# Four eight-product pairs ahead of the first seven-product pair, one behind the last, and variance 1 of the last group's first columns formed on VectorE

## The chip, the cores and the metric

The kernel runs on one core of one Trainium2 chip. The metric is device time in microseconds (us) of the whole launch. The profiler's trace comes from one execution.

## The reference

A batch of 1024 x 10240 values is split in two halves of 5120 columns. Each half goes through two linear layers with layer norm and a leaky ReLU; the two results are put side by side, go through a third such layer, and a last product gives one number per row.

```python
F = 5120
x1, x2 = (x[:, :F], x[:, F:])                      # x: (1024, 10240)
h1 = leaky_relu(layer_norm(x1 @ W1.T))             # W1: (256, 5120)
h2 = leaky_relu(layer_norm(x2 @ W1.T))
h1 = leaky_relu(layer_norm(h1 @ W2.T))             # W2: (64, 256)
h2 = leaky_relu(layer_norm(h2 @ W2.T))
h = jnp.concatenate([h1, h2], axis=-1)
h = leaky_relu(layer_norm(h @ W3.T))               # W3: (8, 128)
return h @ W4.T                                    # W4: (1, 8)
```

`leaky_relu(x) = max(0.05 x, x)`; `layer_norm` subtracts the row's mean and divides by its root of the variance. The first layer is nearly all of the work.

## The kernel before, in words

**Tiling.** The rows are handled in two groups (`g` 0 and 1) of 512 rows, and a group in two batches (`b` 0 and 1) of 256 rows; with both column halves a batch is 512 columns of the moving operand (NC). The 5120 features are 20 pairs of 2 x 128. A product is 128 x 128 weights by 128 x 512 columns, accumulated in one of eight PSUM banks.

**Units.** A unit is one pair of features of one group. An ordinary unit (kind E) has eight products: two halves c (`parts`, buffers E0 and E1, of two blocks of x each) by two batches by two blocks of outputs. A seven (kind S) does a 2 x 2 block product with seven products, three on raw blocks of x (part R) and four on sums of blocks (part T). H and L are E units whose halves use the buffer T; F is the first E of group 1; D is the last two E units together. The string `ORDER` gives the kinds in order for each group; `plan()` numbers the units and their parts.

**Three passes.** Each product is done in three matmuls, since x and the weights are split in a high part (rounded to fp32r) and a low part (the rest): lo x hi, hi x lo, hi x hi. So an E unit is 24 matmuls, an S unit 21. ScalarE makes the high parts (`hi`, L587; weights in L547 and L571), VectorE the low parts (`lo`, L705; weights in L727 and L713). TensorE first takes the high x high products of a part, then waits for the low part.

**Weights.** Weights are read once, in group 0 (and for the two sevens more that group 1 has, nth 12 and 13). ScalarE takes their mean (L541, two for a unit), centres them (L547, two), and for a seven VectorE forms four sums (L739, L744, L749) before ScalarE casts `ws_hi` (L571) and VectorE makes `ws_lo` (L713). A ring of three slots takes the raw weights, so weight n + 3 is loaded after weight n is used up.

**x.** Halves of E units are loaded into a ring of four slots (`load_half`, L406), raw blocks of sevens into a ring of two (L379). The sums of a seven's x (L760, L770, L776) are made on VectorE; for the third to the sixth seven, a DMA that adds makes two of them.

**Order.** Every engine runs its instructions in the order in which they are written. The loop over `RUNS` writes it: a run `es` is the units between one seven and the next, `n` is the seven that follows, `after` the next run. For the first run (`i == 0`) the order is written apart, and also for the run that crosses from group 0 to group 1 (`crosses`). SP's loads are in the same order, each waiting for the low part that frees its slot; a few loads at the start are written out by hand.

**Ends.** After the last unit of a group layer 1 is leaked and squared on ScalarE, squares are summed over the two output blocks on VectorE (`sum_squares`, L834; `sum_last_squares`, L829), and layer 2 follows on TensorE (L1128). In group 1 four small matmuls (eight records, L1141, `sum_variance1`) with a vector of ones sum the squares over partitions, so that the variance has rows on partitions. For batch 0 they stand between layer 2 of batch 0 and TensorE's last block of batch 1 (`last_two`). `variance1` takes the reciprocal and a copy of that, `variance2` forms var12 = var2 x (1/var1) x var1 (L843, L844), GpSimd the power of -1/2 (`root12`, L484), `layer3` the third layer and its variance (L855, L857), GpSimd `root3` (L489), then `layer4` and the output. For group 0 the variances travel by GpSimd's DMAs (L505 to L526), and its end on VectorE stands where `first_end` says, within the sevens of group 1.

## Time and profile before

| | us |
|---|---|
| median of 3 runs | 232.28 |
| lowest and highest | 231.49, 232.99 |
| the profiled execution | 232.81 |
| its span in the trace | 231.0 |
| TensorE busy in it | 224.3 |
| VectorE busy | 191.1 |
| ScalarE busy | 151.7 |

The trace's times count from the span's start. What lies around the span is 232.81 - 231.0 = 1.8 us. In the trace PE is TensorE's matmuls and PEld its weight loads, DVE is VectorE, ACT ScalarE, POOL GpSimd, SP the engine that issues most DMAs. A matmul's end is modelled and overlaps with its successor, so starts are compared, not ends. The granted clock of TensorE is 0.99 of its full 2.4 GHz over the span.

### The profile page before, as it was taken

What the parts mean: (1) busy time and instruction counts of PE and PEld (TensorE: products, weight loads), DVE (VectorE), ACT (ScalarE), POOL (GpSimd) and SP (SyncE); (2) the same over time, 40 slices, a digit from 0 to 9 for tenths busy, and PEclk for the clock granted to TensorE, in tenths of its full rate; (3) what the DMA queues carried; (4) which work ended last, traced back from release to release, by engine and by line L of the source; (5) the groups of instructions that cost most, each with busy time, mean ns of one, the idle gap of its engine ahead of it and who ended that gap; (6) DMA issues with size and microseconds to landing.
All of it is one profiled execution on the core that took longest, in us unless ns stands there. A gap on an engine that the chain in (4) does not pass through costs nothing.

```text
span 231.0 us, 2894 instructions
## 1 busy us (share of the span) xinstructions
PE 224.3 (97%) x999; PEld 179.2 (78%) x999; DVE 191.1 (83%) x245; ACT 151.7 (66%) x240; POOL 28.8 (12%) x41
## 2 busy tenths in 40 slices
PE   8999999999999999999999999999999999999991
PEld 3678776888888888888878888888888878888771
DVE  4589999968869999996669699999989699979324
ACT  5797989779498598963688363665546484824630
POOL 0000020020200200000012243237001400000014
PEclk9999999999999999999999999999999999999996
DMA  6999999999999999556738958668776414150000
GB/s 201 390 407 403 378 318 281 335 289 348 319 234 348 276 295 301 184 166 226 275 65 235 296 176 269 220 208 224 246 246 245 139 74 131 53 182 1 3 0 1
DMA packets 17950, 51.93 MB, mean 225 GB/s; under 512 B 2772, under 2 KB 3156, under 8 KB 17936
## 3 DMA queue, kind: packets, MB, share of 16 engines
q1 hardware_dynamic: 15920, 48.60, 61.5%
q0 software_dynamic: 1872, 2.89, 7.7%
q10 hardware_dynamic: 144, 0.26, 0.3%
q8 instruction: 8, 0.13, 0.3%
q14 instruction: 6, 0.05, 0.1%
HBM read 50.95 MB, written 0.01 MB: 221 GB/s over the span
## 4 chain that ended last, share of the span: by engine, by line
PE 82%; DMA 5%; DVE 4%; ACT 4%; issue 1%; POOL 1%; SPq 1%; POOLq 0%; DVEq 0%
PE acc L1006 79%; DMA xe_raw<-x 5%; PE acc L1128 2%; DVE xe_lo L705 2%; ACT xe_hi L587 2%; ACT unused L541 1%; DVE x_sum L760 1%; PE acc L1141 1%; ACT xt_hi L587 1%; DVE x_sum L770 1%; ACT we_hi L547 0%; POOL inv L484 0%; ACT stage L547 0%; PE acc L1149 0%; PE acc L1157 0%
## 5 line engine op out<-in xcount | busy, mean ns | idle before, releaser
L1006 PE MATMUL acc<-xe_lo,we_hi 128*128 128x512 f32 x176 | 68.9, 391 | 0.3 <-DVE xe_lo L705 0.2
L1006 PE MATMUL acc<-xe_hi,we_lo 128*128 128x512 f32 x176 | 68.6, 390 | 0.0
L705 DVE TENSOR_TENSOR xe_lo<-xe_raw,xe_hi 128x1024 fp32r<-128x1024 f32 (+1 forms) x48 | 55.5, 1177 | 14.5 <-ACT xe_hi L587 14.5
L587 ACT CAST xe_hi<-xe_raw 128x1024 fp32r<-128x1024 f32 (+1 forms) x48 | 47.9, 1010 | 29.5 <-PE acc L1006 22.1
L1006 PE MATMUL acc<-xe_hi,we_hi 128*128 128x512 f32 x176 | 48.3, 391 | 0.0
L1006 PEld LDWEIGHTS acc<-xe_lo,we_hi 128*128 128x128 f32 x176 | 33.1, 188 | 8.4 <-issue 1.7
L1006 PEld LDWEIGHTS acc<-xe_hi,we_hi 128*128 128x128 f32 x176 | 32.9, 188 | 7.4 <-issue 0.7
L1006 PEld LDWEIGHTS acc<-xe_hi,we_lo 128*128 128x128 f32 x176 | 33.1, 188 | 6.7
L587 ACT CAST xt_hi<-x_sum 128x2048 fp32r<-128x2048 f32 x14 | 26.8, 1911 | 12.7 <-DVE x_sum L776 12.7
L705 DVE TENSOR_TENSOR xt_lo<-x_sum,xt_hi 128x2048 fp32r<-128x2048 f32 x14 | 32.0, 2288 | 1.9 <-ACT xt_hi L587 1.9
L1006 PE MATMUL acc<-xt_lo,ws_hi 128*128 128x512 f32 x64 | 25.0, 391 | 0.1
L1006 PE MATMUL acc<-xt_hi,ws_lo 128*128 128x512 f32 x64 | 24.9, 390 | 0.0
L705 DVE TENSOR_TENSOR xr_lo<-xs_raw,xr_hi 128x1536 fp32r<-128x1536 f32 x14 | 24.5, 1751 | 0.0
L587 ACT CAST xr_hi<-xs_raw 128x1536 fp32r<-128x1536 f32 x14 | 20.7, 1476 | 5.8 <-PE acc L1006 5.8
L1006 PE MATMUL acc<-xt_hi,ws_hi 128*128 128x512 f32 x64 | 17.1, 390 | 0.0
L1006 PE MATMUL acc<-xr_lo,ws_hi 128*128 128x512 f32 x42 | 16.6, 396 | 0.0
L1006 PE MATMUL acc<-xr_hi,ws_lo 128*128 128x512 f32 x42 | 16.4, 390 | 0.0
L571 ACT CAST ws_hi<-stage 128x896 fp32r<-128x896 f32 x8 | 7.6, 946 | 12.7 <-DVE stage L749 12.7
L541 ACT ACTIVATE unused<-stage 128x256 bf16<-128x256 f32 x39 | 15.8, 407 | 0.0
L1006 PEld LDWEIGHTS acc<-xt_lo,ws_hi 128*128 128x128 f32 x64 | 12.0, 188 | 3.2 <-issue 0.5
L1006 PEld LDWEIGHTS acc<-xt_hi,ws_hi 128*128 128x128 f32 x64 | 11.9, 188 | 2.7 <-issue 0.2
L496 POOL DMA_DIRECT2D x_sum<-x x4 | 5.0, 1256 | 71.7 <-DMA x_sum<-x 71.7
(107 smaller groups left out, 274.1 us busy)
## 6 DMA issues: line engine op xcount, KB each, us to landing
xe_raw<-x SPq DMA_DIRECT2D x51, 512.0 KB, 5.0
xs_raw<-x SPq DMA_DIRECT2D x14, 768.0 KB, 5.8
stage<-w SPq DMA_DIRECT2D x21, 256.0 KB, 5.8
x_sum<-x SPq DMA_DIRECT2D x10, 256.0 KB, 3.9
x_sum<-x SPq DMA_DIRECT2D x4, 512.0 KB, 4.2
x_sum<-x POOLq DMA_DIRECT2D x4, 512.0 KB, 8.8
stage<-w SPq DMA_DIRECT2D x2, 128.0 KB, 3.1
xe_raw<-x ACTq DMA_DIRECT2D x1, 256.0 KB, 3.2
```

Of the source, the lines that this page charges most:

```text
L496: pool.dma_start(x_sum[:, s, 0:2 * NC].rearrange("p (a n) -> p a n", a=2), b12_of(u).rearrange("p (o n) -> p o n", o=1).broadcast_to([P, 2 ...
L541: act.activation(unused[:, c, :], w_raw[:, s, c * N1:(c + 1) * N1], ACT.Copy, scale=-1.0 / N1, accum_out=w_mean[:, u.pair, c:c + 1]).then_ ...
L571: act.copy(ws_hi[:, u.pair, :], w_mid[:, P:]).then_inc(w_hi_ready, 1)
L587: act.copy(hi_of(u, part), raw_of(u, part)).then_inc(hi_ready[part.buffer], 1)
L705: dve.tensor_tensor(lo_of(u, part), raw_of(u, part), hi_of(u, part).bitcast(F32), ALU.subtract)\
L760: dve.tensor_tensor(x_sum[:, s, 0:2 * NC].rearrange("p (a n) -> p a n", a=2), raw[:, 0:3:2, :], b12, ALU.add).then_inc(two_sums_made, 1)
L770: dve.tensor_tensor(x_sum[:, s, 2 * NC:3 * NC], x_sum[:, s, 0:NC], x_block(u, 2), ALU.add)\
L1006: return pe.matmul(acc[:, bank, :], w, x, start=first, stop=True, skip_group_check=True)
L1128: ins = pe.matmul(h2_ps[b][h * N2:(h + 1) * N2, :], w2_sb[:, m, :], a1[:, b, m, h * T * P:(h + 1) * T * P], start=(m == 0), stop=(m == M - ...
L1141: ins = pe.matmul(acc[:, var1_bank[g][b], k:k + 1], sq1_sum[b][:, j * P:(j + 1) * P], ones[:], start=True, stop=True)
```

## The change

It does four things.

1. Group 0 runs E H E E S E E S ... S E L instead of E H E S E E S ... S E E L: one eight-product unit moves from behind the last seven to ahead of the first. ScalarE, VectorE and SP are written to match; the run that crosses the groups is one unit shorter. The load of w2, w3, w4 goes with its unit (W23_UNIT).
2. `first_end`, the end of group 0 on VectorE, moves one run earlier (SEVEN + 4 instead of SEVEN + 5).
3. In group 1, batch 0, the sums of squares over partitions leave TensorE: VectorE transposes blocks of 32 x 32, reduces over 32, moves the quarters side by side, reduces them, and takes reciprocal and product.
4. var12 = var2 x `cancelled`, where `cancelled` = (1/var1) x var1 is formed ahead. In layer 3 a square with accumulated output for each of the column tiles replaces a square and a reduce.

```diff
-W23_UNIT = 7
-ORDER = ("EHE" + "SEE" * 3 + "SE" * 2 + "SEEL", "FE" + "SE" * 8 + "D")
+W23_UNIT = 8
+ORDER = ("EHEE" + "SEE" * 3 + "SE" * 2 + "SEL", "FE" + "SE" * 8 + "D")
...
             load_w_after(UNITS[1])
             load_halves(UNITS[1], 0)
             load_halves(UNITS[1], 1)
-            load_seven(1)
-            load_two(1)
             load_w_after(UNITS[2])
             load_halves(UNITS[2], 0)
             load_halves(UNITS[2], 1)
+            load_seven(1)
+            load_two(1)
+            load_w_after(UNITS[3])
+            load_halves(UNITS[3], 0)
+            load_halves(UNITS[3], 1)
...
                     if i == 0:
                         hi(es[2], es[2].parts[0])
+                        start_w(es[3])
                         hi(es[2], es[2].parts[1])
                         start_w(n)
                     hi(n, n.parts[0])
-                    for j, u in enumerate(es[1:] if i else [], 1):
+                    for j, u in enumerate(es[1:] if i else es[3:], 1):
...
+            def cancel(a, b):
+                dve.tensor_tensor(cancelled[:, a * J:b * J], var1_inverse[:, a * J:b * J], var1[:, a * J:b * J], ALU.mult)\
+                    .then_inc(cancelled_ready, 1)
+
+            def variance1_of_first_columns():
+                turned = h1[0][1]
+                dve.wait_ge(sq1_summed, B * (GROUPS - 1) + 1)
+                step(dve.transpose(turned, sq1_sum[0]))
+                step(dve.tensor_reduce(quarter_sums[:], turned.rearrange("p (n f) -> p n f", f=Q32), AX.X, ALU.add))
+                for q in range(4):
+                    ins = dve.tensor_copy(side_by_side[:, :, q], quarter_sums[q * Q32:(q + 1) * Q32, :])
+                step(ins)
+                for q in range(4):
+                    rows = side_by_side[:].rearrange("p (h t r) q -> p h t r q", h=H, t=T)[:, :, :, q, :]
+                    ins = dve.tensor_reduce(var1[q * Q32:(q + 1) * Q32, 0:J].rearrange("p (t h) -> p h t", t=T), rows,
+                                            AX.X, ALU.add)
+                step(ins)
+                step(dve.reciprocal(var1_inverse[:, 0:J], var1[:, 0:J]))
+                cancel(0, 1)
...
             def variance2(n, a, b, summed):
-                step(dve.tensor_tensor(var2[:, a * J:b * J], summed, var1_inverse[:, a * J:b * J], ALU.mult))
-                dve.tensor_tensor(var12[:, a * J:b * J], var2[:, a * J:b * J], var1[:, a * J:b * J], ALU.mult)\
+                dve.wait_ge(cancelled_ready, n)
+                dve.tensor_tensor(var12[:, a * J:b * J], summed, cancelled[:, a * J:b * J], ALU.mult)\
                     .then_inc(var12_ready, 1)
...
-                step(dve.scalar_tensor_tensor(out=sq3[:, t], in0=h3[:, t], scalar=1.0 / N3, in1=h3[:, t],
-                                              op0=ALU.mult, op1=ALU.mult))
-                dve.tensor_reduce(var3[:, t], sq3[:, t], AX.X, ALU.add).then_inc(var3_ready, 1)
+                for k in range(a * T, b * T):
+                    ins = dve.scalar_tensor_tensor(out=sq3[:, k], in0=h3[:, k], scalar=1.0 / N3, in1=h3[:, k],
+                                                   op0=ALU.mult, op1=ALU.mult, accum_out=var3[:, k:k + 1])
+                ins.then_inc(var3_ready, 1)
...
                     seven_into(g, 0)
+                    lo(es[1], es[1].parts[0])
                     seven_into(g, 1)
-                    w_lo(es[2])
-                    lo(es[1], es[1].parts[0])
+                    lo(es[1], es[1].parts[1])
                     seven_into(g, 2)
                     seven_into(g, 3)
-                    lo(es[2], es[2].parts[0])
-                    lo(es[1], es[1].parts[1])
-                    lo(es[2], es[2].parts[1])
-                    for part in es[3].parts:
-                        lo(es[3], part)
+                    for part in es[2].parts:
+                        lo(es[2], part)
...
                     lo(es[1], es[1].parts[1])
                     lo(es[2], es[2].parts[0])
+                    w_lo(es[3])
                     lo(es[2], es[2].parts[1])
                     sums(n)
+                    lo(es[3], es[3].parts[0])
                     lo(n, n.parts[0])
+                    lo(es[3], es[3].parts[1])
...
-                first_end = n.nth == SEVEN + 5
+                first_end = n.nth == SEVEN + 4
...
             sum_squares(g, 0)
-            variance1(1, 0, 1, var1_ps(g, 0, 1))
+            variance1_of_first_columns()
             sum_last_squares()
             dve.wait_ge(var2_summed, 1)
             variance2(2, 0, 1, var2_ps(g, 0, 1))
-            variance1(2, 1, 2, var1_ps(g, 1, 2))
+            variance1(1, 1, 2, var1_ps(g, 1, 2))
...
                     if m == 0:
                         layer2(u.g, 0, range(M))
-                        sum_variance1(u.g, 0)
```

**The order near the start.** VectorE's rows from the low part of the third unit's first half (xe0_lo) on, first of the kernel before; L739, L760, L744, L770, L749 and L776 are the sums for the first seven, xr_lo and xt_lo its low parts.

```order
L705 TENSOR_TENSOR xe0_lo<-xe_raw,xe0_hi 128x1024
L705 TENSOR_TENSOR xe1_lo<-xe_raw,xe1_hi 128x1024
L739 TENSOR_TENSOR stage<-stage 128x256
L760 TENSOR_TENSOR x_sum<-xs_raw,x_sum 128x1024
L744 SCALAR_TENSOR_TENSOR stage<-stage 128x128
L770 TENSOR_TENSOR x_sum<-x_sum,xs_raw 128x512
L749 TENSOR_TENSOR stage<-stage 128x128
L776 TENSOR_TENSOR x_sum<-x_sum,xs_raw 128x512
L705 TENSOR_TENSOR xr_lo<-xs_raw,xr_hi 128x1536
L713 TENSOR_TENSOR ws_lo<-stage,ws_hi 128x896
L705 TENSOR_TENSOR xt_lo<-x_sum,xt_hi 128x2048
L727 SCALAR_TENSOR_TENSOR we_lo<-stage,w_mean,we_hi 128x256 x2
```

And of the changed kernel, where L710 is L705, L732 is L727, L744 to L781 the sums:

```order
L710 TENSOR_TENSOR xe0_lo<-xe_raw,xe0_hi 128x1024
L732 SCALAR_TENSOR_TENSOR we_lo<-stage,w_mean,we_hi 128x256 x2
L710 TENSOR_TENSOR xe1_lo<-xe_raw,xe1_hi 128x1024
L744 TENSOR_TENSOR stage<-stage 128x256
L765 TENSOR_TENSOR x_sum<-xs_raw,x_sum 128x1024
L749 SCALAR_TENSOR_TENSOR stage<-stage 128x128
L775 TENSOR_TENSOR x_sum<-x_sum,xs_raw 128x512
L754 TENSOR_TENSOR stage<-stage 128x128
L781 TENSOR_TENSOR x_sum<-x_sum,xs_raw 128x512
L710 TENSOR_TENSOR xe0_lo<-xe_raw,xe0_hi 128x1024
L710 TENSOR_TENSOR xr_lo<-xs_raw,xr_hi 128x1536
L710 TENSOR_TENSOR xe1_lo<-xe_raw,xe1_hi 128x1024
```

The fourth unit's weight part (L732 x2) comes between the third unit's halves; its own low parts (the second xe0_lo and xe1_lo) stand behind the first seven's sums, and with the seven's raw low part between them. Before, they stood behind all of that seven. ScalarE at the same place, before (L541 means, L547 centring, L587 casts of x, L571 cast of a seven's weights):

```order
L587 CAST xe0_hi<-xe_raw 128x1024
L587 CAST xe1_hi<-xe_raw 128x1024
L541 ACTIVATE unused,w_mean<-stage 128x256 x2
L547 ACTIVATE stage<-stage,w_mean 128x256 x2
L587 CAST xr_hi<-xs_raw 128x1536
L571 CAST ws_hi<-stage 128x896
L587 CAST xt_hi<-x_sum 128x2048
L541 ACTIVATE unused,w_mean<-stage 128x256 x2
```

and in the changed kernel (L548, L554, L594, L578):

```order
L594 CAST xe0_hi<-xe_raw 128x1024
L548 ACTIVATE unused,w_mean<-stage 128x256 x2
L554 ACTIVATE we_hi<-stage,w_mean 128x256 x2
L594 CAST xe1_hi<-xe_raw 128x1024
L548 ACTIVATE unused,w_mean<-stage 128x256 x2
L554 ACTIVATE stage<-stage,w_mean 128x256 x2
L594 CAST xr_hi<-xs_raw 128x1536
L594 CAST xe0_hi<-xe_raw 128x1024
L578 CAST ws_hi<-stage 128x896
L594 CAST xt_hi<-x_sum 128x2048
L594 CAST xe1_hi<-xe_raw 128x1024
```

The fourth unit's means and centrings come ahead of xe1_hi of the third, and its casts xe0_hi and xe1_hi before and behind the first seven's ws_hi and xt_hi.

**The end of group 0 on VectorE.** Before, around L966 to L869, with the seven of new weights (L739 to L713) behind it:

```order
L864 TENSOR_TENSOR weighted<-a3,w4_sb 128x32
L865 TENSOR_REDUCE y_sum<-weighted 128x4
L705 TENSOR_TENSOR xe1_lo<-xe_raw,xe1_hi 128x1024
L869 TENSOR_TENSOR y<-y_sum,inv3 128x4
L739 TENSOR_TENSOR stage<-stage 128x256
L760 TENSOR_TENSOR x_sum<-xs_raw,x_sum 128x1024
L744 SCALAR_TENSOR_TENSOR stage<-stage 128x128
L770 TENSOR_TENSOR x_sum<-x_sum,xs_raw 128x512
L749 TENSOR_TENSOR stage<-stage 128x128
L776 TENSOR_TENSOR x_sum<-x_sum,xs_raw 128x512
L705 TENSOR_TENSOR xr_lo<-xs_raw,xr_hi 128x1536
L713 TENSOR_TENSOR ws_lo<-stage,ws_hi 128x896
```

In the changed kernel the same rows, y (L900) and what is behind it, up to the seven with new weights (L744):

```order
L896 TENSOR_REDUCE y_sum<-weighted 128x4
L710 TENSOR_TENSOR xe1_lo<-xe_raw,xe1_hi 128x1024
L900 TENSOR_TENSOR y<-y_sum,inv3 128x4
L765 TENSOR_TENSOR x_sum<-xs_raw,x_sum 128x1024
L775 TENSOR_TENSOR x_sum<-x_sum,xs_raw 128x512
L781 TENSOR_TENSOR x_sum<-x_sum,xs_raw 128x512
L710 TENSOR_TENSOR xr_lo<-xs_raw,xr_hi 128x1536
L710 TENSOR_TENSOR xt_lo<-x_sum,xt_hi 128x2048
L710 TENSOR_TENSOR xe0_lo<-xe_raw,xe0_hi 128x1024
L710 TENSOR_TENSOR xe1_lo<-xe_raw,xe1_hi 128x1024
L744 TENSOR_TENSOR stage<-stage 128x256
L765 TENSOR_TENSOR x_sum<-xs_raw,x_sum 128x1024
```

A seven without weight rows and its eight now stand between the two.

**The last block.** TensorE between the two last blocks, before (L1128 layer 2, L1141 the variance sums):

```order
L1006 MATMUL acc<-xe1_lo,we_hi 128x512
L1006 MATMUL acc<-xe1_hi,we_lo 128x512
L1128 MATMUL acc<-x_sum,w2_sb 64x256 x4
L1141 MATMUL acc<-ones,stage 128x1 x4
L1006 MATMUL acc<-xe0_hi,we_hi 128x512
L1006 MATMUL acc<-xe0_lo,we_hi 128x512
```

and in the changed kernel (L1159 layer 2, L1038 products):

```order
L1038 MATMUL acc<-xe1_lo,we_hi 128x512
L1038 MATMUL acc<-xe1_hi,we_lo 128x512
L1159 MATMUL acc<-x_sum,w2_sb 64x256 x4
L1038 MATMUL acc<-xe0_hi,we_hi 128x512
L1038 MATMUL acc<-xe0_lo,we_hi 128x512
L1038 MATMUL acc<-xe0_hi,we_lo 128x512
```

The row of four matmuls with the vector of ones is gone. VectorE behind the last sum of squares (L834), before:

```order
L834 TENSOR_TENSOR stage<-stage 128x512
L838 RECIPROCAL var1_inverse<-acc 128x4
L839 COPY var1<-acc 128x4
L829 TENSOR_TENSOR stage<-stage,xs_raw 128x256 x2
L843 TENSOR_TENSOR var2<-acc,var1_inverse 128x4
L844 TENSOR_TENSOR var12<-var2,var1 128x4
L838 RECIPROCAL var1_inverse<-acc 128x4
L839 COPY var1<-acc 128x4
L843 TENSOR_TENSOR var2<-acc,var1_inverse 128x4
L844 TENSOR_TENSOR var12<-var2,var1 128x4
L852 TENSOR_TENSOR half3<-acc,inv12 128x32
```

and in the changed kernel (L839):

```order
L839 TENSOR_TENSOR stage<-stage 128x512
L859 STREAM_TRANSPOSE stage<-stage 128x512
L860 TENSOR_REDUCE quarter_sums<-stage 128x16
L862 COPY side_by_side<-quarter_sums 32x16 x4
L866 TENSOR_REDUCE var1<-side_by_side 32x2x2 x4
L869 RECIPROCAL var1_inverse<-var1 128x4
L850 TENSOR_TENSOR cancelled<-var1_inverse,var1 128x4
L834 TENSOR_TENSOR stage<-stage,xs_raw 128x256 x2
L874 TENSOR_TENSOR var12<-acc,cancelled 128x4
L843 RECIPROCAL var1_inverse<-acc 128x4
L844 COPY var1<-acc 128x4
L850 TENSOR_TENSOR cancelled<-var1_inverse,var1 128x4
```

The transpose, the reduces and the copies stand where the reciprocal and copy of batch 0 stood, and each var12 has one row instead of two.

## Rows read from the trace of the kernel before

**Rows 1.** The page, part 1: engine, busy us, share of the span, instructions.

```profile
PE 224.3 (97%) x999; PEld 179.2 (78%) x999; DVE 191.1 (83%) x245; ACT 151.7 (66%) x240; POOL 28.8 (12%) x41
```

**Rows 2.** The chain that ended last, its end: start us, us, engine and line.

```profile
217.36 1.01 PE acc L1128 x8
218.38 0.98 PE acc L1141 x8
...
225.44 0.17 DVE var L843
...
225.63 0.17 DVE var L844
...
225.88 1.01 POOL inv L484
```

**Rows 3.** Timeline of TensorE, 22 to 41: start, us, engine, line, op, shapes [idle].

```profile
23.20 0.84 PE L1006 MATMUL acc<-xr_hi,ws_hi 128*128 128x512 f32 x3
...
28.27 1.07 PE L1006 MATMUL acc<-xe_hi,we_hi 128*128 128x512 f32 x4
...
30.99 1.07 PE L1006 MATMUL acc<-xe_hi,we_hi 128*128 128x512 f32 x4
...
34.99 0.47 PE L1006 MATMUL acc<-xe_lo,we_hi 128*128 128x512 f32 x1 [0.22 <-DVE xe_lo L705]
...
40.17 0.84 PE L1006 MATMUL acc<-xr_hi,ws_hi 128*128 128x512 f32 x3
```

**Rows 4.** Waits of PEld: for what, us, times, longest.

```profile
PEld acc L1006 <- DVE ws_lo L713: 0.8, 2, 0.4
```

**Rows 5.** Timeline of ScalarE, 15 to 24.

```profile
16.40 0.41 ACT L541 ACTIVATE unused<-stage 128x256 bf16<-128x256 f32 x1
...
18.01 1.47 ACT L587 CAST xr_hi<-xs_raw 128x1536 fp32r<-128x1536 f32 x1
20.74 0.94 ACT L571 CAST ws_hi<-stage 128x896 fp32r<-128x896 f32 x1 [1.25 <-DVE stage L749]
21.58 1.91 ACT L587 CAST xt_hi<-x_sum 128x2048 fp32r<-128x2048 f32 x1
```

**Rows 6.** Issue of weight 4; landing (us) of the weights issued at 11.34, 18.32.

```profile
11.34 0.42 SPq L370 DMA_DIRECT2D stage<-w  x1
...
DMA to landing us min/median/max: 7.3/7.3/7.3
...
DMA to landing us min/median/max: 9.3/9.3/9.3
```

**Rows 7.** Timeline of VectorE, 17 to 35.

```profile
18.14 0.42 DVE L739 TENSOR_TENSOR stage<-stage 128x256 f32<-128x256 f32 x1 [0.33 <-ACT stage L547]
...
21.22 1.75 DVE L705 TENSOR_TENSOR xr_lo<-xs_raw,xr_hi 128x1536 fp32r<-128x1536 f32 x1
...
33.63 1.22 DVE L705 TENSOR_TENSOR xe_lo<-xe_raw,xe_hi 128x1024 fp32r<-128x1024 f32 x1
```

**Rows 8.** Timelines of VectorE and GpSimd, 177 to 184.

```profile
177.28 0.20 DVE L966 RECIPROCAL var_inverse<-var 128x8 f32<-128x8 f32 x1
...
183.28 0.42 DVE L739 TENSOR_TENSOR stage<-stage 128x256 f32<-128x256 f32 x1
...
178.02 2.52 POOL L484 TENSOR_TENSOR inv<-var,minus_half 128x8 f32<-128x8 f32 x1 [17.96 <-DVE var L844]
```

**Rows 9.** Timeline of VectorE, 217 to 228.

```profile
217.33 0.69 DVE L834 TENSOR_TENSOR stage<-stage 128x512 f32<-128x512 f32 x1 [1.74 <-ACT stage L609]
...
223.03 0.91 DVE L829 TENSOR_TENSOR stage<-stage,xs_raw 128x256 f32<-128x256 f32 x2 [3.40 <-ACT xs_raw L690]
...
227.42 0.18 DVE L855 SCALAR_TENSOR_TENSOR sq<-h 128x16 f32<-128x16 f32 x1
227.63 0.17 DVE L857 TENSOR_REDUCE var<-sq 128x2 f32<-128x16 f32 x1
```

**Rows 10.** Groups by line and form: busy us, mean ns | idle before.

```profile
L541 ACT ACTIVATION_READ_ACCUMULATOR unused<-stage 128x1 f32 x39 | 7.3, 187 | 0.0
```

More of the change, by code:

```diff
@@ L30 @@
 LEAK = 0.05
+Q32 = 32
 WARM_UP = 9
@@ L206, in rec_kernel @@
         var1_inverse = sb("var1_inverse", [P, B * J])
-        var2 = sb("var2", [P, B * J])
+        cancelled = sb("cancelled", [P, B * J])
+        quarter_sums = sb("quarter_sums", [P, NC // Q32])
+        side_by_side = sb("side_by_side", [Q32, NC // Q32, 4])
         var12 = sb("var12", [P, B * J])
@@ L282, in rec_kernel @@
         var1_copied = sem("var1_copied")
+        cancelled_ready = sem("cancelled_ready")
         small_copied = sem("small_copied")
@@ L641, in _ @@
                     copy_p1(es[0].g)
-                    start_w(es[2])
-                    for k in range(2):
-                        for u in es[1:3]:
-                            hi(u, u.parts[k])
+                    for u in es[1:3]:
+                        for part in u.parts:
+                            hi(u, part)
+                    layer1_end(es[0].g)
                     for part in es[3].parts:
                         hi(es[3], part)
-                    layer1_end(es[0].g)
-                    for part in es[4].parts:
-                        hi(es[4], part)
                     for b in range(B):
@@ L668, in _ @@
                         hi(u, u.parts[1])
-                    if i == 0 or len(es) == 1:
+                    if len(es) == 1:
                         end_w(n)
@@ L934, in _ @@
                         sum_squares(g, b)
-                    for part in es[4].parts:
-                        lo(es[4], part)
+                    for part in es[3].parts:
+                        lo(es[3], part)
                     sums(n)
@@ L966, in _ @@
                     step(dve.reciprocal(var1_inverse[:], var1[:]))
+                    cancel(0, B)
                     dve.wait_ge(small_copied, 1)
-                    variance2(B, 0, B, small[:, 0:B * J])
+                    variance2(1, 0, B, small[:, 0:B * J])
                 w_lo(after[0])
```

1 line of the change is left out of this document (added).

## The prediction

> **What bounds the kernel now.** First the page's busy times: TensorE is busy 97% of the span and VectorE 83% [rows 1]. A busy TensorE says little by itself, so the second view is the chain of waits, read at its end. There the chain is TensorE's in one piece until 225.4 us: layer 2 of batch 0 (L1128), then eight records of the variance sums (L1141, 0.98 us), then the last products. After it come two VectorE products, a root on GpSimd, and small steps [rows 2]. Work that leaves TensorE in this stretch is worth its own time, if nothing else comes due first.
>
> Third, the starts of TensorE's groups near the beginning. Twelve matmuls of an eight-product half take 2.72 us (28.27 to 30.99), so one takes 0.227. From the raw group of the first seven (23.20) to that of the second (40.17) lie 21 + 48 = 69 matmuls, which need 15.64 us; they take 16.97 [rows 3]. So 1.33 us are lost there. The same comparison elsewhere, on the rows of the same view, finds about 0.09 us in each later group of one seven and two eights. Last, the waits of weight loads name VectorE's ws_lo twice, 0.8 us in all [rows 4]: one is at 24 us (in the raw group that starts at 23.20), the other at 189 us, at the first seven of group 1 that brings new weights.
>
> The number of products and DMAs does not change, so the sum has four terms: the head, the place of group 0's end on VectorE, the removed sums, the shorter chain.
>
> **Head.** Group 0 now runs E H E E before its first seven S. What the order buys S0 is 5.44 us of TensorE (24 matmuls) ahead of it. What it asks: the fourth unit's x halves, which before were used after S0, are used before it. They keep their places in the DMA queue, so their casts must get past S0's work on ScalarE and VectorE, and there the new order puts S0's sums ahead of them. I follow that chain.
>
> ScalarE: two means and two centrings of one unit's weights take 1.61 us (16.40 to 18.01, [rows 5]). The fourth unit's now stand ahead of the third unit's second cast, which was through at 16.40 and is now through by about 18; TensorE wants it 12 matmuls ahead of S0, at 23.20 - 2.72 = 20.5. Then S0's means need weight 4, which lands at 11.34 + 7.3 = 18.64 [rows 6]. Before, S0's weights were number 3 and long there. So S0's means begin at 18.66 and the raw cast 1.61 later, at 20.27. Before, that cast began at 18.01 and VectorE's sums at 18.14 [rows 5, 7]; the 0.13 between them kept, the sums now begin at 20.40.
>
> VectorE: sums of weights and x take 18.14 to 21.22, 3.08 us [rows 7], now to 23.48. Only then comes xe0_lo of the fourth unit. In the old trace xe_lo at 33.63 let TensorE go on at 34.99, 1.36 us later [rows 3, 7]; now 24.84. TensorE, at 23.20 with the high product, would take it at 23.20 + 0.91 = 24.11. Lost: 0.73, and 0.08 for the restart.
>
> Second half of that unit: ws_hi began 2.60 us behind the first sum (20.74 against 18.14), so at 23.00, xt_hi 0.84 later (20.74 to 21.58). That cast is busy 1.91, so xe1_hi begins at about 25.65 and is through some 1.05 later, at 26.70 [rows 5, 7]. TensorE, with the first half done at 24.84 + 0.08 + 1.81 = 26.73, gets it just in time, but the low part, which VectorE begins at 26.74, frees TensorE at 28.10 against 27.64. Lost: 0.46 + 0.08. Together 1.35 us.
>
> After S0 the extra unit is in hand. VectorE has for an eight two low parts of 1.22 and two weight parts of about 0.4, some 3.2 us, against 5.44 on TensorE, and the stalls ahead of the second seven shrink to the usual 0.09. So 1.44 us are lost where 1.33 were. Where the groups change, about 0.06 us that stood at the end of the old order's extra eight fall away. **Head: +0.05**, nothing within the error. Its bounds: -1.0 if the two stalls vanish but the rest holds, +1.3 if weight 4 is late (rivals).
>
> **Group 0's end on VectorE.** The reciprocal and products of group 0's variance, its layers 3 and 4, now stand one seven and one eight earlier: 45 matmuls, 10.2 us. Before, this stretch with the two low parts of its eight took 177.28 to 183.28, 6.0 us [rows 8]; without the ending, two low parts and a short wait for a cast, some 3.3. It stood directly ahead of the seven with new weights, whose ws_lo is the second wait of [rows 4]. Now the surplus of 2.7 us falls on a seven without weight work (no weight sums, no ws_lo: about 2 us less for VectorE), where [rows 4] has no wait. The sums for the new weights begin about a microsecond earlier, and the stall goes, by matmul starts 0.26 us. The variance rows come by GpSimd's DMAs, and GpSimd had issued the last of them 18.0 us before its root at 178.02 [rows 8], so they are there 10 us earlier too. **-0.26** (+0.3, if the surplus shows there, to -0.3).
>
> **Removed sums.** Eight records L1141, 218.38 to 219.36, stand alone on TensorE between layer 2 and the last block [rows 2]. Switching from layer 2 to the products costs a little either way. Everything behind waits for TensorE's last block: ScalarE's activations, sum_last_squares, layer 2 of batch 1. **-0.98** (bounds -0.8, where the switch grows, and -1.05).
>
> What covers the replacement: VectorE's time from the end of sum_squares (217.33 + 0.69 = 218.02) to sum_last_squares, at 223.03 before, 222.05 now [rows 9], so 4.0 us. The trace has no transpose. From below a 128x512 operation of 0.69 bounds it, from above one of 128x1024 with 1.22 [rows 7, 9]; nearest is the same shape. The reduce over 512 values: the same bounds. Four copies and four reduces on 32 partitions: each between 0.10 (overlapped) and 0.22 (waiting for the one ahead). Reciprocal and product: 0.40. With 0.73 + 0.73 + 8 x 0.18 + 0.40 it is 3.3 us, covered with 0.7 to spare; the high end, 1.26 + 1.26 + 1.76 + 0.40 = 4.7, would overrun by 0.7.
>
> The Trainium skill (VectorE: DVE Perf Modes, Two Vector instructions with no wait between them) says that an instruction starting in another group of 32 partitions than its predecessor is held until that has finished. By that rule the eight small ones cost the full 0.18 to 0.22 each; the cover would still hold. No row here shows such a pair.
>
> **Shorter chain.** var12 is one product instead of two: L843 at 225.44, L844 at 225.63, the root at 225.88 [rows 2]. The quotient var1/var1 is formed ahead, while TensorE does variance 2. **-0.19.** In layer 3 a square and a reduce took 227.42 to 227.80, 0.38 us [rows 9]; now two squares with an accumulated output. If they overlap wholly, -0.2. If each also reads out an accumulator as ScalarE's does, 187 ns a time [rows 10], unhidden, 2 x 0.18 + 2 x 0.19 = 0.73, +0.35. ScalarE's reads overlap about half. I take **+0.05**.
>
> The same page and section of the Trainium skill counts an operation with accumulated output as two instructions, the main one and a read. By that the pair would end about 0.1 us later than before instead of 0.05.
>
> **Sum.** +0.05 - 0.26 - 0.98 - 0.19 + 0.05 = -1.33 us: span 231.0 to 229.7, and that execution 232.81 to 231.5. It was itself 0.5 us above the median of 232.28, so the median goes to **231.0**.
>
> **Rivals.**
> 1. *The new stalls don't come, the head gains.* If the fourth unit's low parts come 0.7 us earlier (sooner landing of weight 4, ScalarE waits only for that), the head loses some 0.4 instead of 1.4: 230.0. For it: ScalarE is done with the third unit by about 18 and waits for nothing but that weight. Against: the weight's place in the queue is unchanged. 0.15.
> 2. *Weight 4 lands late, slower than before.* Each microsecond adds one to the wait for xe0_lo. A weight issued at 18.32 into the full queue took 9.3 us [rows 6]; with that, 2.0 more: 233.0. It decides from 1.3 us of extra delay on. Against: nothing ahead of it in the queue moves. 0.06.
> 3. *The replacement on VectorE overruns its cover.* Sum_last_squares, var12 and all behind come later one for one. At the high end 0.7, 231.7; if the transpose took four passes, 2.1 more, the whole gain of 0.98 and more: 232.4. 0.14.
> 4. *The reordering costs elsewhere* (the group change has one eight fewer as cover): about 1 us, 232.0. Against: no view names a wait of TensorE for VectorE's low parts there. 0.06.
>
> The forecast has 0.59, with a range of its own of 230.4 to 231.6. For 8 in 10: **230.0 to 232.2**. A measurement of this kernel tells about 1%, 2.3 us, from no change. Faster by over that needs nearly rival 1 and every other term at its good end, or something not seen: 0.10. Slower, rival 2 and more: 0.05. Within: 0.85.
>
> **What would show it.** Head: TensorE waits on VectorE's xe_lo near 24.1 to 24.8 and 27.6 to 28.1, none on ws_lo at 24, none of size near 35 and 38. Sums on VectorE starting at 20.4. No wait on ws_lo near 189. At the end layer 2 followed directly by L1038, the transpose near 0.69, the cancelled product ready before 222.05 (by the shifted clock), one product ahead of each root. Wrong would be: a wait of sum_last_squares on VectorE's own chain, a transpose above 1.4 us, S0's sums at 22 or later.

## The result, and the profile after

The changed kernel takes 230.13 us (median of 12 runs, 229.87 to 231.62) where the kernel before takes 231.53 in the same comparison (12 runs, 231.37 to 232.99): a ratio of 0.9936, with a 95% interval of 0.992 to 0.9953. That is 1.40 us less, a real gain that is smaller than the 1% that the prediction counts as faster. The forecast of "the same within 1%", with a sum of -1.33 us, holds. Its 231.0 us was counted from a median of three runs, 232.28, which more runs put at 231.53; counted from that, it would have said 230.2. So 230.13 lies inside the range for 8 in 10 (230.0 to 232.2) by only 0.13 us, and below the forecast's own 230.4 to 231.6: the starting median was 0.75 us too high.

The profiled execution of the changed kernel took 230.18 us, its span 228.4 (before: 231.0). First the page, part 1 (engine, busy us, share of the span, instructions), beside [rows 1]:

```profile
PE 222.0 (97%) x991; PEld 178.7 (78%) x991; DVE 193.6 (85%) x264; ACT 151.9 (66%) x240; POOL 27.9 (12%) x41
```

TensorE has eight instructions fewer, VectorE 19 more and 2.5 us more work. TensorE was still the engine that everything stood behind. The chain that ended last, after the change (start us, us, what; "x" is the number of instructions):

```profile
10.03 7.36 DMA stage<-w
...
17.41 0.91 ACT unused L548 x4
18.32 0.81 ACT stage L554 x2
...
22.32 1.15 DVE xe_lo L710
23.46 0.14 issue
23.60 3.16 PE acc L1038 x12
26.76 0.10 issue
26.85 90.79 PE acc L1038 x398
117.65 1.88 PE acc L1159 x16
...
215.90 1.01 PE acc L1159 x8
216.91 2.99 PE acc L1038 x12
...
221.57 1.00 PE acc L1172 x8
222.57 0.02 issue
222.59 0.18 DVE var_inverse L843
...
223.37 1.01 POOL inv L491
...
226.05 0.16 DVE y L900
```

Two things are to be seen. In [rows 2] layer 2 of batch 0 (L1128) was followed by eight records of the sums (L1141, 0.98 us); here layer 2 (L1159, at 215.90) is followed at once by the products of the last block (L1038, at 216.91). And at the start the chain now runs through weight 4, ScalarE's means and VectorE's sums to xe_lo, the path that the prediction followed, 1.3 us earlier than it said.

Of these 1.3 us none comes from the change. In the profile before, ScalarE could cast the second half of the very first input only at 8.04 us and TensorE lost 1.0 us behind it, in the steps that start at 7.85 and 8.80; after the change the cast came at 6.72 and this stop is missing. The code up to there is the same. Experiments 1 and 2 show that it comes and goes with the execution: in the second of them the kernel before issues weight 4 at 10.12 us, not at 11.34.

So single spans (231.0 against 228.4, 2.6 us) mislead, and the comparison is made by stretches that this start doesn't touch. This table is worked out from the timelines of TensorE, with the trace's spans to the hundredth: up to its first row of layer 2 in group 0 (L1128 at 118.73 before, L1159 at 117.58 after), from there to layer 2 of batch 0 in group 1 (217.29 and 215.83), and from there to the end of the span. "Late" is what TensorE lost behind the late second half of the first input; "-" means no such stop. The numbers in brackets are those of the experiments.

| profile | late | to layer 2, group 0 | group 1 | end | span |
|---|---|---|---|---|---|
| before | 1.00 | 118.73 | 98.56 | 13.72 | 231.01 |
| before again (1) | 0.89 | 118.04 | 98.57 | 13.72 | 230.33 |
| before, third (2) | - | 117.25 | 98.55 | 13.72 | 229.52 |
| new order alone (3) | - | 117.41 | 98.64 | 13.72 | 229.77 |
| new ends alone (4) | - | 117.36 | 98.26 | 12.55 | 228.17 |
| **changed** | - | 117.58 | 98.25 | 12.56 | 228.39 |
| sums on TensorE again (5) | - | 117.76 | 98.25 | 13.42 | 229.43 |
| group 0's end as before (6) | - | 117.60 | 98.70 | 12.55 | 228.85 |
| chain doubled (7) | 0.56 | 118.09 | 98.26 | 12.81 | 229.16 |
| square and reduce (8) | - | 117.31 | 98.25 | 12.68 | 228.24 |
| weight first (9) | - | 116.28 | 98.25 | 12.56 | 227.09 |
| low parts moved (10) | - | 115.97 | 98.25 | 12.55 | 226.77 |

Where the code of the stretch is the same, the column of group 1 repeats within 0.1 us and that of the end within 0.01. The column up to layer 2 of group 0 scatters by 0.2 us or more, also without the late start.

The tail on VectorE after the change, to set beside [rows 9] (timeline: start us, us, engine, line, operation, shapes, count, [idle before and what ended it]):

```profile
215.86 0.69 DVE L839 TENSOR_TENSOR stage<-stage 128x512 f32<-128x512 f32 x1 [1.74 <-ACT stage L616]
216.59 0.71 DVE L859 STREAM_TRANSPOSE stage<-stage 128x512 f32<-128x512 f32 x1
217.34 0.69 DVE L860 TENSOR_REDUCE quarter_sums<-stage 128x16 f32<-128x512 f32 x1
218.06 0.72 DVE L862 COPY side_by_side<-quarter_sums 32x16 f32<-32x16 f32 x4
218.81 0.68 DVE L866 TENSOR_REDUCE var<-side_by_side 32x4 f32<-32x16 f32 x4
219.53 0.18 DVE L869 RECIPROCAL var_inverse<-var 128x4 f32<-128x4 f32 x1
219.74 0.16 DVE L850 TENSOR_TENSOR cancelled<-var_inverse,var 128x4 f32<-128x4 f32 x1
220.63 0.98 DVE L834 TENSOR_TENSOR stage<-stage,xs_raw 128x256 f32<-128x256 f32 x2 [0.73 <-ACT xs_raw L695]
...
224.91 0.17 DVE L886 SCALAR_TENSOR_TENSOR sq<-h 128x8 f32<-128x8 f32 x1
225.00 0.08 DVE L886 DVE_READ_ACCUMULATOR sq<-h 128x1 f32 x1
225.00 0.16 DVE L886 SCALAR_TENSOR_TENSOR sq<-h 128x8 f32<-128x8 f32 x1
225.09 0.08 DVE L886 DVE_READ_ACCUMULATOR sq<-h 128x1 f32 x1
225.09 0.18 DVE L893 SCALAR_TENSOR_TENSOR a<-h 128x32 f32<-128x32 f32 x1
```

From the transpose (216.59) to the end of the cancelled quotient (219.90) lie 3.31 us, the 3.3 of the prediction. Behind it VectorE has 0.73 us with nothing to do before sum_last_squares (L834), so the new work is covered.

### The profile page after: what moved, and what is told of

Same layout as the page of the kernel before. It is cut to its first block, busy times and chain, and to the rows that moved or that the text cites. A ratio compares the mean times of both kernels' runs of the same rounds, so it can differ in the third digit from the quotient of the medians.

```text
span 228.4 us, 2897 instructions
## 1 busy us (share of the span) xinstructions
PE 222.0 (97%) x991; PEld 178.7 (78%) x991; DVE 193.6 (85%) x264; ACT 151.9 (66%) x240; POOL 27.9 (12%) x41
## 4 chain that ended last, share of the span: by engine, by line
PE 87%; DMA 5%; DVE 2%; ACT 2%; POOL 1%; issue 1%; SPq 1%; POOLq 0%; DVEq 0%
PE acc L1038 84%; DMA stage<-w 3%; DMA xe_raw<-x 2%; PE acc L1159 2%; ACT unused L548 1%; DVE x_sum L765 1%; DVE xe_lo L710 1%; ACT xe_hi L594 0%; POOL inv L491 0%; PE acc L1172 0%; DVE ws_lo L732 0%; ACT stage L554 0%; PE acc L1188 0%; POOLq L157 0%; POOL inv L496 0%
## 5 line engine op out<-in xcount | busy, mean ns | idle before, releaser
L1038 PE MATMUL acc<-xe_lo,we_hi 128*128 128x512 f32 x176 | 68.8, 391 | 0.8 <-DVE xe_lo L710 0.7
L1038 PE MATMUL acc<-xe_hi,we_lo 128*128 128x512 f32 x176 | 68.6, 390 | 0.0
L594 ACT CAST xe_hi<-xe_raw 128x1024 fp32r<-128x1024 f32 (+1 forms) x48 | 48.1, 1010 | 25.3 <-PE acc L1038 23.4
L710 DVE TENSOR_TENSOR xe_lo<-xe_raw,xe_hi 128x1024 fp32r<-128x1024 f32 (+1 forms) x48 | 55.3, 1178 | 10.6 <-ACT xe_hi L594 10.4
L1038 PE MATMUL acc<-xe_hi,we_hi 128*128 128x512 f32 x176 | 48.4, 391 | 0.0
L1038 PEld LDWEIGHTS acc<-xe_lo,we_hi 128*128 128x128 f32 x176 | 33.0, 188 | 8.8 <-issue 2.1
L1038 PEld LDWEIGHTS acc<-xe_hi,we_hi 128*128 128x128 f32 x176 | 32.9, 188 | 7.8 <-issue 1.1
L1038 PEld LDWEIGHTS acc<-xe_hi,we_lo 128*128 128x128 f32 x176 | 33.0, 188 | 6.7
L594 ACT CAST xt_hi<-x_sum 128x2048 fp32r<-128x2048 f32 x14 | 26.7, 1910 | 16.5 <-DVE x_sum L781 16.5
L710 DVE TENSOR_TENSOR xt_lo<-x_sum,xt_hi 128x2048 fp32r<-128x2048 f32 x14 | 32.0, 2289 | 1.9 <-ACT xt_hi L594 1.9
L1038 PE MATMUL acc<-xt_lo,ws_hi 128*128 128x512 f32 x64 | 25.0, 390 | 0.0
L1038 PE MATMUL acc<-xt_hi,ws_lo 128*128 128x512 f32 x64 | 24.9, 389 | 0.0
L710 DVE TENSOR_TENSOR xr_lo<-xs_raw,xr_hi 128x1536 fp32r<-128x1536 f32 x14 | 24.5, 1753 | 0.0
L594 ACT CAST xr_hi<-xs_raw 128x1536 fp32r<-128x1536 f32 x14 | 20.7, 1478 | 5.4 <-PE acc L1038 5.4
L1038 PE MATMUL acc<-xt_hi,ws_hi 128*128 128x512 f32 x64 | 17.1, 389 | 0.0
L548 ACT ACTIVATE unused<-stage 128x256 bf16<-128x256 f32 x39 | 15.8, 407 | 1.7 <-DMA stage<-w 1.7
L1038 PE MATMUL acc<-xr_hi,ws_lo 128*128 128x512 f32 x42 | 16.4, 389 | 0.0
L1038 PE MATMUL acc<-xr_lo,ws_hi 128*128 128x512 f32 x42 | 16.4, 389 | 0.0
L1038 PEld LDWEIGHTS acc<-xt_lo,ws_hi 128*128 128x128 f32 x64 | 12.0, 188 | 2.8 <-issue 0.4
L765 DVE TENSOR_TENSOR x_sum<-xs_raw,x_sum 128x1024 f32<-128x1024 f32 x10 | 12.2, 1221 | 2.4 <-DMA x_sum<-x 2.4
L1038 PEld LDWEIGHTS acc<-xt_hi,ws_hi 128*128 128x128 f32 x64 | 12.0, 188 | 2.5
```

The source lines that it names most:

```text
L548: act.activation(unused[:, c, :], w_raw[:, s, c * N1:(c + 1) * N1], ACT.Copy, scale=-1.0 / N1, accum_out=w_mean[:, u.pair, c:c + 1]).then_ ...
L594: act.copy(hi_of(u, part), raw_of(u, part)).then_inc(hi_ready[part.buffer], 1)
L710: dve.tensor_tensor(lo_of(u, part), raw_of(u, part), hi_of(u, part).bitcast(F32), ALU.subtract)\
L765: dve.tensor_tensor(x_sum[:, s, 0:2 * NC].rearrange("p (a n) -> p a n", a=2), raw[:, 0:3:2, :], b12, ALU.add).then_inc(two_sums_made, 1)
L1038: return pe.matmul(acc[:, bank, :], w, x, start=first, stop=True, skip_group_check=True)
```

## The experiments

The theory (A) is the prediction's: the removed sums and the shorter chain give about 1.1 us, group 0's end 0.3, and the new order of the first units neither gains nor loses. The rival (B) gives part of the gain to the new order, whose start looked 1.3 us earlier in the two first profiles, and calls the end's share about half. Others are named where they come in. Each ratio is taken against runs of the kernel before made beside those of the experiment; their median was 231.49 to 231.52 us.

### 1 and 2. The kernel before, twice more

No edit. What was expected of the first:

> The kernel before, unchanged, timed and profiled once more. The two profiled executions differ by 2.6 us in span, of which 1.3 lie ahead of 22 us: in the old trace the second half of the first x pair reached ScalarE at 8.04, in the new one at 6.72. Theory A: that is chance of the execution, the change has no part in it. Then the ratio is 1.000 within 0.3%, and the profile shows the cast either near 6.7 (span about 229.7) or near 8.0 (span 231). Theory B: the order of the kernel before makes it land late. Then its profile again shows 8.0, and the ratio says nothing.

Measured: 231.73 us (11 runs), ratio 1.0012 (0.9995 to 1.0029); the profiled execution took 232.13 with a span of 230.3. ScalarE's timeline has the second cast of the first pair late again:

```profile
7.66 1.14 ACT L587 CAST xe_hi<-xe_raw 128x512 fp32r<-128x512 f32 x2 [1.40 <-DMA xe_raw<-x]
```

Twice in two profiles of before, and never in those of the changed kernel and of six relatives: that looked like a property of the kernel, until a derivative of the changed kernel (experiment 7) had it too. So the kernel before was profiled a third time, with this expectation:

> The kernel before once more, for one profile. In both of its profiles so far TensorE stood idle twice in the start, near 7.6 to 7.9 and 8.3 to 8.8 us, for the second half of the first pair's input, and in one of a derivative of the changed kernel too (0.29 and 0.27 us); the other derivatives and the changed kernel do not show it. Theory A: it is chance of the execution, the code up to there being the same in all of them. Then this profile may as well show none of it, and its span is about 229.7 to 230.0 us; if it shows it, 230.3 to 231.0. Theory B: it belongs to this kernel, for a reason not seen yet, and is there a third time, with a span of 230.3 or more.

It took 231.33 us, its span was 229.5, and ScalarE's timeline reads:

```profile
6.82 1.14 ACT L587 CAST xe_hi<-xe_raw 128x512 fp32r<-128x512 f32 x2 [0.56 <-DMA xe_raw<-x]
```

So the lateness belongs to the execution, not to the kernel. The transfer is issued at 2.09 to 2.12 us in all three; why it lands up to 1.2 us later in some executions stays open.

This third profile also corrects the baseline of the head. The five stops of TensorE near 32 to 37 us lose 0.34, 0.08, 0.06, 0.35 and 0.08 us there, 0.91 together. The 0.26 at 24 us, which the prediction counted among its 1.33, is missing from it. It is missing from the profile of experiment 1 too, which started late like the first, so the late start alone does not make it; what does stays open.

### 3 and 4. The new order alone, and the new ends alone

Kernel 3 is the kernel before with the new order of units. These lines and those that follow from them (the loads, the casts, the low parts):

```diff
-W23_UNIT = 7
+W23_UNIT = 8
-ORDER = ("EHE" + "SEE" * 3 + "SE" * 2 + "SEEL", "FE" + "SE" * 8 + "D")
+ORDER = ("EHEE" + "SEE" * 3 + "SE" * 2 + "SEL", "FE" + "SE" * 8 + "D")
```

> The kernel before with the new order of units alone (head and group change), the end of group 0 on VectorE, the sums on TensorE, the two products and the reduce of layer 3 as before. Theory A (head neutral): within 0.2 us of before, ratio 1.000 to 1.001; VectorE's low parts of the fourth unit stop TensorE for 1.4 us, the later stops go. The wait on ws_lo near 189 stays. Theory B (the order brings the gain): about 1 us faster, ratio 0.995.

Measured: 231.68 us (12 runs), ratio 1.0012 (1.0 to 1.0024). The new order costs 0.2 us or nothing; it gains nothing. The wait for ws_lo near 188 us is still there (0.4 us), as expected. Kernel 4 is the complement: the order of before, with the variance on VectorE, the cancelled quotient, the accumulated squares, and group 0's variance taken at the same distance from the end of the group (`first_end` at `SEVEN + 4`).

> The kernel before with the ends of the change alone: the last first columns' variance on VectorE, the cancelled sum, the squares with their sum in one instruction, and group 0's last block laid out as in the changed kernel; the order of the head's units stays that of before. It is the complement of the kernel with the new order alone, which took 1.0012 of the time before. Theory A: the new order of the head is neutral (plus 0 to 0.2 us), so this one carries the whole gain: a ratio of 0.992 to 0.995, as fast as the changed kernel or 0.1 to 0.2 us faster; the head shows the stops of before (1.2 to 1.4 us), the tail those of the changed kernel. Theory B: the new order saves something that shows only together with the ends (the place of the weights of the products behind it, say), so this gives about half, a ratio near 0.997.

Measured: 229.99 us (5 runs), ratio 0.9932 (0.9918 to 0.9946). This carries the whole gain and is 0.14 us ahead of the changed kernel, within what the runs can tell. Rival B falls. TensorE's timeline of kernel 3 shows why the order is worth nothing:

```profile
21.82 1.07 PE L1030 MATMUL acc<-xe_hi,we_hi 128*128 128x512 f32 x4
23.46 0.47 PE L1030 MATMUL acc<-xe_lo,we_hi 128*128 128x512 f32 x1 [0.58 <-DVE xe_lo L710]
...
25.46 1.17 PE L1030 MATMUL acc<-xe_hi,we_hi 128*128 128x512 f32 x4
26.72 0.47 PE L1030 MATMUL acc<-xe_lo,we_hi 128*128 128x512 f32 x1
```

Four matmuls take 0.91 us and the next starts 1.64 and 1.26 behind the start of the four: 0.73 and 0.35 us lost. The stops near 35 and 38 of before have moved to 23 and 26.

### 5. The sums back on TensorE

```diff
-            variance1_of_first_columns()
+            variance1(1, 0, 1, var1_ps(g, 0, 1))
...
-            variance1(1, 1, 2, var1_ps(g, 1, 2))
+            variance1(2, 1, 2, var1_ps(g, 1, 2))
...
                     if m == 0:
                         layer2(u.g, 0, range(M))
+                        sum_variance1(u.g, 0)
```

> The changed kernel with the variance sums of group 1, batch 0 on TensorE again, as before; all else changed. Theory A: they cost 0.9 us of TensorE alone, so this is 0.9 us slower than the changed kernel and about 0.5 faster than before, ratio 0.998. Theory B (the chain after the last block sets the end, TensorE's time there is not what counts): as fast as the changed kernel, ratio 0.994.

Measured: 231.36 us (12 runs), ratio 0.9997 (0.9976 to 1.0018), 1.2 us above the changed kernel. Its runs spread from 230.86 to 232.90, so the profile is the better witness: by spans it is 1.04 us longer, of which the last stretch has 0.86 (13.42 against 12.56) and the scatter of the first 0.18. The chain has the sums again:

```profile
217.10 0.98 PE acc L1173 x8
218.08 2.87 PE acc L1038 x12
```

The twelve products behind them take 2.87 us here and 2.99 without the sums. That 0.12 is what the switch from layer 2 straight to the products costs more than the one from the sums to the products; the prediction named it and set it at nothing. 0.98 less 0.12 is the 0.86 of the stretch.

### 6. Group 0's end one unit later again

```diff
-                first_end = n.nth == SEVEN + 4
+                first_end = n.nth == SEVEN + 5
```

> The changed kernel with the end of group 0 on VectorE back at its old place, one seven later. Theory A: TensorE waits again for ws_lo near 187, 0.26 us by matmul starts, and the kernel is 0.3 us slower than the changed one. Theory B (something else in the change removed the wait): no wait there and the same time.

Measured: 230.71 us (10 runs), ratio 0.9954 (0.9933 to 0.9975), 0.58 above the changed kernel; in the stretch of group 1, 98.70 against 98.25, so 0.45. By TensorE's starts 0.36 of it is lost at one place, the raw group of the first seven with new weights (187.21 to 188.48). The waits of weight loads name ws_lo again (what is waited for, us in total, times, longest), as [rows 4] did and the changed kernel's do not:

```profile
PEld acc L1038 <- DVE ws_lo L718: 0.5, 1, 0.5
```

The term is real, and of the expected size or somewhat larger.

### 7. How much cover the variance on VectorE has

The transpose and the reduce are done twice.

```diff
+                step(dve.transpose(turned, sq1_sum[0]))
+                step(dve.tensor_reduce(quarter_sums[:], turned.rearrange("p (n f) -> p n f", f=Q32), AX.X, ALU.add))
```

> The changed kernel with the transpose and the reduce behind it made twice, the second time over the same data. In the changed kernel VectorE is idle 0.73 us between cancelled and sum_last_squares. Theory A (cover as read from the trace): 1.43 us more of VectorE, 0.7 of it hidden, the rest on the path: 0.7 us slower than the changed kernel, sum_last_squares starts right behind cancelled. Theory B (the end is set by another chain, VectorE's has more room): the same time.

Measured: 230.28 us (10 runs), ratio 0.9946 (0.993 to 0.9963): 0.15 us above the changed kernel, not 0.7. The last stretch grew by 0.25 (12.81 against 12.56). VectorE's timeline:

```profile
221.73 0.16 DVE L850 TENSOR_TENSOR cancelled<-var_inverse,var 128x4 f32<-128x4 f32 x1
221.81 0.75 DVE L834 TENSOR_TENSOR stage<-stage,xs_raw 128x256 f32<-128x256 f32 x2
```

The chain grew by 1.47 us (two more operations, 218.57 to 220.04) and sum_last_squares followed it without a gap. But TensorE wants the first half of sum_last_squares only behind layer 2 of batch 1, for the last sums over partitions. They start here at

```profile
222.28 1.05 PE L1174 MATMUL acc<-ones,stage 128*128 128x1 f32 x8 [0.19 <-DVE stage L834]
```

and in the changed kernel, without a wait, at

```profile
221.50 1.05 PE L1172 MATMUL acc<-ones,stage 128*128 128x1 f32 x8
```

That is 1.59 and 1.33 us behind the start of layer 2 of batch 1 (220.69 and 220.17), so 0.26 us is passed on. In the changed kernel the first half is done near 220.97 (220.63 and the 0.34 that the chain of this run gives it) and TensorE comes for it 0.5 us later. The idle 0.73 us ahead of L834 was thus not the whole cover: it is 1.47 - 0.26, about 1.2 us. The expectation took the start of sum_last_squares for the moment at which it is wanted.

### 8. Square and reduce instead of accumulated squares

```diff
-                for k in range(a * T, b * T):
-                    ins = dve.scalar_tensor_tensor(out=sq3[:, k], in0=h3[:, k], scalar=1.0 / N3, in1=h3[:, k],
-                                                   op0=ALU.mult, op1=ALU.mult, accum_out=var3[:, k:k + 1])
-                ins.then_inc(var3_ready, 1)
+                step(dve.scalar_tensor_tensor(out=sq3[:, t], in0=h3[:, t], scalar=1.0 / N3, in1=h3[:, t],
+                                              op0=ALU.mult, op1=ALU.mult))
+                dve.tensor_reduce(var3[:, t], sq3[:, t], AX.X, ALU.add).then_inc(var3_ready, 1)
```

> The changed kernel with layer 3's square and reduce as before instead of two squares with accumulated output. Theory A: from the start of the square to the end of the variance 0.38 us instead of the 0.26 read in the changed kernel, 0.12 us slower, within the error of the timing; the trace decides. Theory B (accumulated output gives nothing, the root on GpSimd is what waits): y starts at the same distance from the last root.

Measured: 230.06 us (6 runs), ratio 0.9934 (0.9913 to 0.9954). The times can't tell it from the changed kernel. The profile can: from the root of the variances to the start of the last product 2.81 us pass (223.09 to 225.90), against 2.68 in the changed kernel (223.37 to 226.05). The accumulated form is 0.13 us shorter, and the last stretch 0.12 (12.56 against 12.68).

### 9. Weight 4 loaded ahead of the first seven's x

```diff
+            load_w_after(UNITS[1])
             load_seven(0)
             load_two(0)
-            load_w_after(UNITS[1])
```

> The changed kernel with weight 4 loaded ahead of the first seven's x instead of behind it. Theory A (the sums wait for ScalarE's centring, and that for weight 4's landing at 17.4): means begin at about 16.4, the sums 0.9 us earlier, TensorE's first stop (0.82 us) goes, the second shrinks to at most 0.35, in all 0.9 us faster than the changed kernel, ratio to before 0.990. Theory B (the x halves or the chain of casts behind it set the stop): at most 0.3 us faster, ratio 0.993.

Measured: 229.15 us (5 runs), ratio 0.9892 (0.987 to 0.9913), 0.98 us below the changed kernel. ScalarE's timeline shows what went:

```profile
16.13 0.42 ACT L548 ACTIVATE unused<-stage 128x256 bf16<-128x256 f32 x1
```

In the changed kernel the means of S0's weights (the first seven's) began at 17.41 behind a wait of 0.94 for their DMA. Here they begin 1.28 us earlier, behind no wait. TensorE's stop of 0.82 at the first half of the fourth unit is gone, and of the second one 0.30 is left. That is rival 1 of the prediction, made to happen.

### 10. The fourth unit's low parts ahead of the seven's

The landing of the weight can also be left as it is, and the order of work behind it changed. VectorE takes the first low part between the sums instead of behind them, and the second directly behind the last sum, ahead of the seven's own raw low part. ScalarE casts the fourth unit's two halves before it finishes S0's weights (its edit is of the same kind and is not shown):

```diff
-                    sums(n)
+                    w_two_sums(n)
+                    two_sums(n)
                     lo(es[3], es[3].parts[0])
-                    lo(n, n.parts[0])
+                    w_third_sum(n)
+                    third_sum(n)
+                    w_fourth_sum(n)
+                    fourth_sum(n)
                     lo(es[3], es[3].parts[1])
+                    lo(n, n.parts[0])
```

> The changed kernel, with another order around the first seven: ScalarE casts the fourth unit's first half ahead of the seven's raw blocks and the second half ahead of ws_hi; VectorE makes the first low part between the two pairs of sums, and the second ahead of xr_lo. Theory A (the order of the sums ahead of xe0_lo makes the 1.4 us stop): both stops go or stay under 0.2 us, 1.2 us faster than the changed kernel, ratio to before 0.989. Theory B (landing of the x halves or of weight 4 sets it whatever the order): no gain over the changed kernel, ratio 0.994.

Measured: 228.69 us (5 runs, 228.61 to 229.61), ratio 0.9884 (0.9869 to 0.99): the fastest of all, 1.44 us below the changed kernel. Its first chain on TensorE is in one piece:

```profile
5.00 6.64 PE acc L1049 x28
11.64 0.09 issue
11.73 104.31 PE acc L1049 x458
```

and VectorE takes the low part of the fourth unit in the middle of the sums, at 20.46 instead of 22.23:

```profile
19.32 1.22 DVE L771 TENSOR_TENSOR x_sum<-xs_raw,x_sum 128x1024 f32<-128x1024 f32 x1
20.46 1.22 DVE L716 TENSOR_TENSOR xe_lo<-xe_raw,xe_hi 128x1024 fp32r<-128x1024 f32 x1
21.59 0.28 DVE L755 SCALAR_TENSOR_TENSOR stage<-stage 128x128 f32<-128x128 f32 x1
```

Nothing comes due late behind it: from 11.73 on the 458 products run in a row. Kernel 4, the old order with the same ends, took 229.99 us, so the new order with its helpers arranged to suit it is 1.3 us ahead; as the changed kernel has it, the place of a few casts and two low parts hides that. It is the place that matters, not the load of VectorE, which is busy for 193.4 us here and 193.6 in the changed kernel. Not shown is how much a like rearrangement would give to the old order, whose own stops of about 1 us remain, or experiments 9 and 10 together.

## Why the prediction was right, point by point

**Head (+0.05): right in what it found, a little short in size.** This is the part that was followed step by step, and with a common shift of 1.25 to 1.3 us (the late start) each step is found:

| step | predicted | found | difference |
|---|---|---|---|
| S0's means on ScalarE | 18.66 | 17.41 | -1.25 |
| sums on VectorE | 20.40 | 19.15 | -1.25 |
| low part of the fourth unit | 23.48 | 22.23 | -1.25 |
| TensorE goes on, first half | 24.84 | 23.60 | -1.24 |
| TensorE goes on, second half | 28.10 | 26.85 | -1.25 |
| lost in all | 1.35 | 1.41 | |

TensorE's rows behind the last four lines, after the change:

```profile
21.87 1.07 PE L1038 MATMUL acc<-xe_hi,we_hi 128*128 128x512 f32 x4
23.60 0.47 PE L1038 MATMUL acc<-xe_lo,we_hi 128*128 128x512 f32 x1 [0.66 <-DVE xe_lo L710]
...
25.59 1.17 PE L1038 MATMUL acc<-xe_hi,we_hi 128*128 128x512 f32 x4
26.85 0.47 PE L1038 MATMUL acc<-xe_lo,we_hi 128*128 128x512 f32 x1
```

The step that was too good is the other side of the balance, the 1.33 us lost before between the raw groups of the first two sevens. It was taken from one profile. Counted the same way, the second and third profile of before and kernel 4, which has the same order, lose 1.05, 1.04 and 1.21. The head therefore costs rather 0.2: up to layer 2 of group 0 the profiles without the late start reach 117.25 and 117.36 us with the old order, and 117.31 to 117.76 with the new (five, mean 117.53). With a scatter of 0.45 among those five, the 0.2 is a rough size.

**Group 0's end (-0.26): right.** The stretch of group 1 shrank by 0.31 us, and grew by 0.45 when the edit alone was undone. The cause is as named: the wait for ws_lo is gone, and no stop of TensorE takes its place in the stretch.

**Removed sums (-0.98): right, with a smaller size.** Eight records left the chain, and 0.12 came back in the first products behind the switch (2.99 us for twelve instead of 2.87). The stretch shrank by 0.86 (13.42 to 12.56, experiment 5), within the bounds and toward the -0.8 "where the switch grows".

**Cover of the replacement: right.** The transpose took 0.71 us, against 0.73 assumed; the reduce 0.69. The four copies took 0.72 and the four reduces 0.68, so 0.18 and 0.17 each. The Trainium skill (VectorE: DVE Perf Modes, Two Vector instructions with no wait between them) states that an instruction whose input or output starts in another group of 32 partitions than the last one's is held until every earlier VectorE instruction has finished. The trace agrees: these rows step by 0.17 to 0.18, their whole duration, while two products on the same 128 partitions step by 0.09 (225.00 and 225.09 above). No run has the same copies on one group of partitions, so the comparison is between different operations. The cover was understated, 0.7 where experiment 7 gives about 1.2.

**Shorter chain (-0.19 and +0.05): right and wrong.** From the end of the last sums to the root 1.00 us passed (223.39 to 224.39, third profile of before) and 0.80 pass now (222.57 to 223.37): -0.20. The accumulated squares were costed at +0.05 on the pattern of ScalarE's read, 187 ns [rows 10], half hidden. VectorE's read took 0.08 us and lay wholly beside the next instruction, so the pair takes 0.26 (224.91 to 225.17) where square and reduce took 0.38 [rows 9]: -0.12, confirmed by experiment 8. This term had the wrong sign. The same section of the Trainium skill counts an accumulated output as two instructions. The trace agrees on that; the prediction's estimate from it, 0.1 us later than before, is not found, since the second instruction is hidden.

**Sum.** By the stretches +0.23 - 0.31 - 1.16 = -1.24 us, by the medians -1.40, predicted -1.33. The 1.16 of the end is made up of 0.86 for the sums, 0.20 for the product and 0.12 for the squares. Errors of opposite sign cancelled: the head was too good by 0.18 and the switch by 0.12, the squares too bad by 0.17 and group 0's end by 0.05. The sum is thus right to a tenth partly by luck; its terms are right to about 0.2 each.

**Rivals.** Rivals 1 to 3 did not happen, though the measured 230.13 us is near the 230.0 of rival 1; that is the high starting median, not its mechanism. The new stalls came, weight 4 took 7.36 us to land instead of 7.3, and the replacement stayed under its cover. Rival 4, a cost of the reordering elsewhere, left no trace: there was no stop of TensorE above 0.1 us between 27 and 117 us in the changed kernel.

## What to carry to other kernels

When a unit is moved ahead in the order of a busy engine, move its preparation on the helper engines too, past whatever waits for a late transfer: here the order of products alone was worth nothing, and with one low part pulled inside the other unit's sums, one directly behind them, and their casts ahead of the cast of its weights it was worth 1.3 us. Small sums that stand alone on the bounding engine can go to an engine that idles meanwhile; the cover is to be counted to the moment at which the bounding engine takes the result, not to the start of the next operation behind the gap. And a baseline of stops is to be taken from more than one profile, stretch by stretch, because what one execution loses at its start can look like a gain of the change.

## What the runs showed of the hardware

The same transfer, issued within 0.03 us of the same time in the same program, was cast by ScalarE from 8.04, 7.66 and 6.82 us in three executions of the kernel before, and the time of the whole moved with it (232.81, 232.13 and 231.33 us). A transpose of 128x512 f32 on VectorE took 0.71 us, as much as an elementwise operation of that shape (0.69). The read of an accumulator took 0.08 us on VectorE against 0.19 on ScalarE.
